# Both maxima of a step in even slots, the rotation of queries ahead in odd slots, GpSimd's scaling ahead of its normalising

## What is computed

```python
h = tok(x)                           # convolutions, norms, an importance MLP, pooling: (64, 128, 64)
h = h + attention(layernorm(h))      # below
h = h + experts(layernorm(h))        # top 2 of 8 experts, gelu
```

```python
q = rmsnorm(rope(x @ wq.T)) * q_norm_w       # 16 heads
k = rmsnorm(rope(x @ wk.T)) * k_norm_w       # one head
v = x @ wv.T
scores = q @ k.T / sqrt(64)                  # causal, within a window
attn = softmax(scores)
out = (attn @ v) @ wo.T
```

## Time and profile before

| | value |
|---|---|
| median of three runs | 1920.44 us |
| the profiled execution | 1921.04 us |
| its span | 1919.1 us |
| mean granted TensorE clock | 0.981 |
| busy: TensorE, VectorE, ScalarE, GpSimd | 93%, 80%, 71%, 48% of the span |
| attention slots 0 to 255 | about 1033 to 1735 us |

### The profile page before, as it was taken

How to read it: one execution, slowest core, us unless ns; L and a number is a source line. 1 busy time by engine, 2 the same in 40 slices (tenths; PEclk the granted TensorE clock), 3 DMA queues, 4 the chain that set the end, 5 groups by cost and what they waited for, 6 DMA issues and landing times.

```text
span 1919.1 us, 35529 instructions
## 1 busy us (share of the span) xinstructions
PE 1778.8 (93%) x10789; PEld 1275.9 (66%) x10789; DVE 1530.7 (80%) x3377; ACT 1355.5 (71%) x3865; POOL 920.5 (48%) x1544
## 2 busy tenths in 40 slices
PE   3999999999999977999997999999999999989998
PEld 2777887887887866877775666666655665654443
DVE  5788888888888856567657899998999888986665
ACT  1567777677677653444445999999998999986765
POOL 1222322322322310032238999999898999983200
PEclk9999999999999988999997999999999999999999
DMA  3311111111111000000000000000000000004454
GB/s 98 95 44 40 34 45 39 34 45 39 34 45 39 25 1 1 1 1 1 1 1 1 2 2 2 2 2 2 2 2 1 2 2 2 2 7 177 189 216 165
DMA packets 30520, 69.05 MB, mean 36 GB/s; under 512 B 14108, under 2 KB 14748, under 8 KB 28028
## 3 DMA queue, kind: packets, MB, share of 16 engines
q1 hardware_dynamic: 30332, 66.78, 10.6%
HBM read 45.12 MB, written 2.36 MB: 25 GB/s over the span
## 4 chain that ended last, share of the span: by engine, by line
PE 33%; DVE 10%; ACT 9%; issue 6%; POOL 4%; DVEq 0%; ACTq 0%; POOLq 0%
ACT apb L1460 5%; PE ps L65 4%; PE ps L67 3%; PE ps L66 3%; PE ps L1218 3%; PE ps L1777 3%; PE ps L1201 3%; PE ps L1189 3%; PE ps L1228 2%; POOL apb L1574 1%; DVE atq L1281 1%; PE ps L1763 1%; PE ps L1184 1%; DVE amx L1321 1%; ACT aqT L1449 1%
## 5 line engine op out<-in xcount | busy, mean ns | idle before, releaser
L1460 ACT ACTIVATE apb<-ps,amx 128x128 f32<-128x128 f32 x1024 | 360.5, 369 | 23.6 <-DVE amx L1321 22.8
L1574 POOL TENSOR_TENSOR apb<-apb,arc 128x512 f32<-128x512 f32 x256 | 268.2, 1048 | 28.4 <-DVE arc L1329 27.4
L1460 ACT ACTIVATION_READ_ACCUMULATOR apb<-ps,amx 128x1 f32 x1024 | 214.4, 209 | 0.0
L1336 DVE COPY apT<-ps 128x512 f32<-128x512 f32 x256 | 172.6, 674 | 51.2 <-PE ps L1201 47.9
L583 POOL TENSOR_TENSOR h0h<-h0h,const 128x1 fp32r<-128x1 f32 x256 | 46.7, 218 | 338.8 <-DVE h0l L479 338.8
L65 PE MATMUL ps<-h0h,w123h 128*128 128x512 f32 x512 | 203.2, 397 | 0.0
L67 PE MATMUL ps<-h0h,w123l 128*128 128x512 f32 x512 | 202.5, 396 | 0.0
L66 PE MATMUL ps<-h0l,w123h 128*128 128x512 f32 x512 | 202.5, 395 | 0.0
L479 DVE SCALAR_TENSOR_TENSOR h0l<-ps,h0h 128x1024 fp32r<-128x1024 f32 x128 | 156.1, 1219 | 46.5 <-ACT h0h L383 46.5
L1201 PEld LDWEIGHTS ps<-const,apb 128*128 128x128 f32 x1024 | 109.8, 141 | 121.3 <-issue 90.9
L1321 DVE TENSOR_REDUCE amx<-ps 128x4 f32<-128x512 f32 x256 | 174.3, 681 | 4.6 <-PE ps L1189 4.3
(11 more groups left out here) (325 smaller groups left out, 5030.8 us busy)
## 6 DMA issues: line engine op xcount, KB each, us to landing
h<-gates SPq DMA_DIRECT2D x8, 2048.0 KB, 7.0
atq<-gates SPq DMA_DIRECT2D x8, 2048.0 KB, 7.0
x0k<-x0h SPq DMA_DIRECT2D x128, 72.0 KB
x<-in_x SPq DMA_DIRECT2D x32, 192.0 KB, 2.6
x0k<-x0l SPq DMA_DIRECT2D x64, 72.0 KB
x0k<-x0h SPq DMA_DIRECT2D x64, 48.0 KB
out<-akT SPq DMA_DIRECT2D x16, 128.0 KB, 1.9
x0k<-x0l SPq DMA_DIRECT2D x32, 48.0 KB
```

The costliest lines, as they stand in the source:

```text
L1336: ve.tensor_copy(pT[:, 4 * k:4 * k + 4, :], ps[:, TB, :].rearrange("p (h t) -> p h t", h=4)).then_inc(S["pT"], 1)
L1460: last = ac.activation(pb[:, i % 2, head, :], ps[:, SB[n % 3], h * T:(h + 1) * T], ACT.Exp, bias=mx[:, k, h:h + 1], accum_out=sm[:, i % 2, ...
L1574: po.tensor_tensor(p, p, rc[:, i % 2, 4 * k:4 * k + 4].unsqueeze(2).to_broadcast([T, 4, T]), ALU.mult).then_inc(S["pn"], 1)
```

## The change

In the even slots of VectorE the maxima of both parts of the step are issued one after the other, at the head of the slot; the odd slots have none. In the odd slots the rotation of queries stands first, ahead of the reciprocal and `p_copy`. On GpSimd `scale_q` is issued ahead of `normalize` (they meet in even slots alone). Nothing else changes: no instruction, wait, buffer or slot of any other engine.

```diff
             if u == first(0):
                 ve.wait_ge(made["m3"], QUADS)
-            if 0 <= u < PARTS:
+            if u % 2 == 0 and 0 <= u < PARTS:
                 maximum(u)
+                maximum(u + 1)
+            if u in at_q:
+                rope_q(at_q[u])
             if 0 <= u - 1 < PARTS:
                 recip(u - 1)
             if u in at_pt:
                 p_copy(at_pt[u])
-            if u in at_q:
-                rope_q(at_q[u])
             if u - 1 in at_q:
                 sum_q(at_q[u - 1])
...
             if u == first(0):
                 po.wait_ge(made["m3"], QUADS)
+            if u in at_qm:
+                scale_q(at_qm[u])
             if 0 <= u - 1 < PARTS:
                 normalize(u - 1)
             if u in at_q:
                 add_q(at_q[u])
-            if u in at_qm:
-                scale_q(at_qm[u])
```

## The result

The changed kernel takes 1905.85 us (median of 4 runs, 1903.42 to 1908.46) against 1921.01 in the same series: ratio 0.9921, 95% interval 0.9904 to 0.9938. It is faster by 0.8%, 15 us, where the forecast of 1908.5 had 12. The profiled execution took 1905.99 us.

The account below looks back on a forecast made before the run. No engine is full; in attention four nearly full engines wait for each other in turn. Twelve quads at 1.04 us give 12.5, less 0.6 is 11.9: 1909.1 profiled, 1908.5 as median; range 1897 to 1922.

Parts of the forecast that it names:

- A and B: First two steps of a quad, holding the output projection, 11.95 us together; no gain claimed, TensorE running without a gap.
- C to H: The other six steps of a quad; claimed to bring the next quad's first scores 1.04 us earlier.
- E: Fifth step of a quad; the second maximum delays the copy and its transpose, leaving 0.38 of a 0.45 us lead.
- The twelve quads: Attention quads from 1095 to 1617 us, each claimed to save 1.04 us, 12.5 in all.
- The last quads: Two quads with GpSimd also normalising for experts; no saving, later odd part costs 0.3 to 0.9 us, 0.6 taken.
- The first ramp: Start of the attention stage; 0 taken, bounded by a maximum's 0.60 us either way.
- second rival: GpSimd's slack of about 1 us is used up and `p_t` waits about 0.5 a quad; 1914 us, chance 0.11.
- H: Last step of a quad, largest term; odd maximum long done, rotation earlier, lead going from 0.47 to 1.04 us.
- D: Fourth step of a quad; VectorE arrives without the odd slot's maximum, so the next scores come 0.45 us earlier.
- The slower one: Second maximum ahead of `p_copy` becomes the path, costing 0.60 us at E, H and their like; 1937 us, chance 0.14.
- The no-change rival: Next scores wait for TensorE alone in H as in A and B, time moving into its queue; 1920 us, chance 0.12.
- The rule on the drain: VectorE's next operation waits for an empty pipe; copy in E 0.08 us later, 1909.5 us; not used in the forecast.

Follow-up runs that it names:

- e5_split: Changed kernel, but in steps E and H the odd part's maximum stands behind the even slot's reciprocal and copy; 1903.62 us, ratio 0.9905.
- e4_max_rope: Changed kernel with GpSimd's old order, normalising ahead of scaling; 1904.47 us, ratio to the kernel before 0.9914.
- e3_scale: Kernel before with only GpSimd's scaling moved ahead of its normalising; 1920.79 us, ratio 0.9999.
- e7_no_lead_g: Changed kernel, but in the odd slot of the step before H the rotation stands behind reciprocal and copy again; 1904.12 us, ratio 0.9908.
- e8_lead_g_only: Changed kernel with the rotation ahead only in the odd slot of the step before H, elsewhere behind reciprocal and copy; 1921.17 us, ratio 1.0002.
- e12_max_ab: Changed kernel, both maxima together only in A and B; in C to H the odd maximum heads the odd slot, ahead of the rotation; 1912.43 us, ratio 0.9961.
- e1_maxima: Kernel before with only the maxima moved, both into even slots; rotation and GpSimd's order as before; 1921.75 us, ratio 1.0000.

## Why the prediction was right, and where it was not

**A and B**: 5.97 and 5.98, unchanged. Right, in all fourteen kernels.

**C to H**: saved 0.21, 0.35, 0.08, 0.00, 0.11 and 0.55, where the working had 0.17, 0.28, -0.07, 0.02, 0.07 and 0.57. The sum is 1.30 for 1.04, and the period of 42.00 lies just below the 42.2 to 42.4 that was named as the sign of being right. The term that was mis-sized most is E: the copy does come late and the transpose waits, but I charged the path 0.07 for it, while the scores of F come 5.20 after those of E. e5_split puts what the late copy costs there at 0.10; even with it E is 0.08 shorter than before.

**The twelve quads.** The prediction says that only the last full quad differs from a middle one. That was read from too few stretches: four of the twelve were longer before (43.34 to 45.08 us). They gained 0.80, 1.34, 1.57 and 1.53, the one before these 1.23, the other seven about 1.30. That all twelve together gained 15.5, as twelve middle quads would have, is luck.

**The last quads**: 0.65 lost in the last full one; I took 0.6. The closeness is partly luck: GpSimd's order costs 0.93 there, a little above the bound of 0.9 on the expected loss, and VectorE's order, to which I gave nothing, gains 0.28 (e4_max_rope: 44.29). And I gave no gain to the quad before it, since GpSimd has the experts' work there too, and it gained its 1.31: 41.42 of 42.00 us of GpSimd's still fitted. With the 0.26 a quad over twelve quads (3.1), the forecast lacked 4.4; the first ramp and the later start of the attention, below, took 1.3 of it back, and so the profiled execution came out 3.1 us under the 1909.1 of the sum.

**The first ramp**: I took 0; from the first scores to the first output projection it went from 61.19 us before to 61.75, 0.56 lost. In it stands the mechanism of the second rival (a transpose waiting 0.96 for the later normalising). With GpSimd's old order the ramp takes 59.93, so the 0.56 seems to be a gain of 1.26 and a loss of 1.82; but e3_scale, with GpSimd's move alone, lost nothing there, and each is one profile, so the sizes are not shown. Sum of the profiled executions: 12.0 x 1.30 is 15.6, and 1.31, less 0.65 and 0.56, is 15.7; the attention began 0.7 us later than in the profile of before, which leaves 15.0, and the profiled executions differ by 15.05.

**The cause of H** was told wrongly. The size of the term was right (0.57 for 0.55), but I let both waits of ScalarE there be ended by two things at once, the odd maximum's place and the rotation's lead in G. The maxima alone give 0.29 of it; the lead in G's own slot is worth 0.06 (e7_no_lead_g), because rotation and copy only change places as what comes last there, and the remaining 0.2 goes with the leads in other slots (e8_lead_g_only, with the lead in G alone: 5.35, against 5.17 with all). I followed one chain (rotation, `square`, projection) and not the other (copy, transpose) with the rotation put back.

**What the maxima need.** My working of D had VectorE arrive early because the second maximum was hidden in A and B. That holds (e12_max_ab), but only with the rotation ahead: alone the maxima gain nothing. That a reciprocal waits for its exponentials stands in the kernel's own text; I did not draw from it that a lead gained before is lost at such a wait, nor did I in the expectation of e1_maxima, which had a gain of 3 to 6 us.

**The rivals.** The slower one named the right place: transposes do wait for the copy, 42.8 us of weight loads and 11.6 of matmuls, against my mark of 20. It named the wrong price, 0.60 in each of E and H: taking the second maximum out of the copy's way gave 0.10 and 0.31 (e5_split), since in E the scores then wait 0.43 for ScalarE. One argument against it was misread too: of VectorE's 23.5 us of waiting for the transposes, 10.7 and 10.6 lie in A and B, and only 0.2 each in C and F, where the weight loads now wait 7.0 and 5.7 us for the copy. The no-change rival falls with the period, the second (GpSimd) holds only at the two ends: in the middle e3_scale and e4_max_rope show no cost of GpSimd's order.

**The rule on the drain.** The Trainium skill, page "VectorE: DVE Perf Modes", section "The DRAIN you can't avoid", would have the second of two maxima start when the first is done; the pair takes 1.28 us here, with 0.68 for one, so it starts 0.60 later. The trace disagrees with that sentence, as it did before the change. The prediction left out that the same section goes on: "A next op that is not held starts earlier". An earlier start is what the trace shows, so the 1909.5 worked out from the first sentence alone had no ground.

## What to carry to other kernels

Put in front of an in-order queue what is ready, and behind it what waits: a short instruction that waits for another engine (here a reciprocal of 0.17 us) can throw away the lead gained before it, and another reordering may pay only once that wait is filled. Look at such pairs of edits together; here they were worth 0.0 and 0.5 us a period alone and 1.3 together. And where the engine of a wait is not last in its stage, the length of the wait says little of its price: removing a wait of 0.73 us was worth 0.10; of the two waits in H the one of 0.29 went, and the step became 0.31 shorter.

## What was not expected

The start of the attention stage differs by up to 4 us between profiled runs (1032.06 in e3_scale, 1036.06 in e1_maxima), although nothing in front of it was changed and a middle quad repeats to 0.02 us. Why was not looked into.
